# A graph network's softmax stage: ScalarE takes five of ten steps instead of four, and VectorE's product operations stand one by one between the maxima

## The reference

```python
w_m = (efeat @ W_msg + b_msg).reshape(E, 16, 16)
w_a = (efeat @ W_attn + b_attn).reshape(E, 16, 16)
h_src = feat[src][:, :, None]
e1, e2 = w_m * h_src, w_a * h_src
seg_max = segment_max(e2, dst)
ex = exp(e2 - seg_max[dst])
attn = ex / segment_sum(ex, dst)[dst]
ft = segment_sum(e1 * attn, dst).sum(axis=1)
```

## Time and profile before

| | |
|---|---|
| median of three runs | 10487.75 us |
| the profiled execution | 10485.69 us |
| its span, first to last instruction | 10482.2 us |
| busy: TensorE, VectorE, ScalarE, GpSimd | 7697.7, 7480.8, 2810.4, 8040.9 us |
| 1650 gathers `arena<-d_feat` | 3064.6 us, 1857 ns each |
| 990 products, line 1579 | 610.0 us, 678 ns each |
| 1650 forward maxima, line 1525 | 789.3 us, 478 ns each |
| 1485 sums, line 1561 | 1100.8 us, 741 ns each |
| 10560 ScalarE multiplications, line 726 | 1928.6 us, 526 ns each |

### The profile page before, as it was taken

The page is one execution under the profiler, slowest core; times in us unless marked ns, Lnnn a source line. Parts: engine busy times, 40 slices in busy tenths (PEclk is TensorE's granted clock), DMA queues, the critical chain, the costliest instruction groups (busy, mean ns, idle before and its releaser), DMA issues.

```text
span 10482.2 us, 126613 instructions
## 1 busy us (share of the span) xinstructions
PE 7697.7 (73%) x34167; PEld 3938.2 (38%) x34167; DVE 7480.8 (71%) x13704; ACT 2810.4 (27%) x12100; POOL 8040.9 (77%) x5375
## 2 busy tenths in 40 slices
PE   0899984999964666666666666617999993988884
PEld 0455542555532223322222222203555552444442
DVE  2556551444437999999999999974888872777774
ACT  0111111000005666666666666602000000000000
POOL 4788885777767888888888888753888884888887
PEclk6999996999987888887888888857999995988886
DMA  1333331222214666666666666635222221333331
GB/s 36 96 93 99 96 85 31 63 64 64 64 35 122 192 192 191 191 191 191 189 191 190 190 190 189 190 97 188 77 77 77 77 68 41 90 91 92 91 89 44
DMA packets 501017, 1210.69 MB, mean 115 GB/s; under 512 B 244715, under 2 KB 281743, under 8 KB 480135
## 3 DMA queue, kind: packets, MB, share of 16 engines
q1 hardware_dynamic: 241732, 983.55, 28.9%
q0 software_dynamic: 223712, 118.77, 9.2%
q10 hardware_dynamic: 35440, 106.85, 3.2%
HBM read 415.09 MB, written 787.23 MB: 115 GB/s over the span
## 4 chain that ended last, share of the span: by engine, by line
POOL 37%; issue 22%; PE 19%; DVE 14%; ACT 3%; DMA 2%; DVEq 1%; SPq 1%; ACTq 0%; POOLq 0%
POOL arena L513 37%; PE PS L876 11%; DVE arena L1525 4%; DVE arena L1579 4%; PE PS L1010 3%; PE PS L1011 3%; DVE arena L1529 3%; ACT arena L726 2%; DVE arena L1561 2%; PE PS L898 2%; DMA d_rel<-arena 1%; DVE arena L1539 1%; DVEq L1519 1%; DMA d_nn<-arena 0%; SPq L310 0%
## 5 line engine op out<-in xcount | busy, mean ns | idle before, releaser
L876 PE MATMUL PS<-arena,TB 125*128 125x500 bf16 (+1 forms) x17325 | 4102.2, 384 | 140.2 <-DVE arena L1275 138.3
L513 POOL DMA_INDIRECT arena<-d_feat,srci x1650 | 3064.6, 1857 | 557.8 <-issue 496.2
L513 POOL DMA_INDIRECT arena<-d_h,srci x1584 | 2026.2, 1279 | 697.6 <-issue 472.5
L876 PEld LDWEIGHTS PS<-arena,TB 125*128 125x128 bf16 (+1 forms) x17325 | 1570.0, 100 | 2363.7 <-issue 986.2
L726 ACT ACTIVATE arena<-PS,arena 125x32 f32<-125x32 f32 x10560 | 1928.6, 526 | 44.4 <-DMA arena<-d_feat,srci 44.4
L1286 DVE SCALAR_TENSOR_TENSOR arena<-arena,lane,PS 128x500 f32<-128x500 f16 x825 | 598.1, 725 | 1554.5 <-PE PS L876 1059.1
L1010 PE MATMUL PS<-arena,ident 125*125 125x512 f32 x1650 | 1087.8, 747 | 804.1 <-DVE arena L1529 802.5
L513 POOL DMA_INDIRECT arena<-d_rel,irel x858 | 1216.4, 1418 | 422.0 <-issue 261.2
L513 POOL DMA_INDIRECT arena<-d_nn,srci x858 | 1215.9, 1417 | 351.3 <-issue 261.0
L1275 DVE TENSOR_SCALAR arena<-arena,lane 125x1500 bf16<-125x1500 f16 (+1 forms) x1848 | 1188.5, 701 | 187.4 <-PE PS L876 71.8
L1561 DVE SCALAR_TENSOR_TENSOR arena<-arena 125x512 f32<-125x512 f32 x1485 | 1100.8, 741 | 0.3
(11 more groups left out here) (262 smaller groups left out, 5722.0 us busy)
## 6 DMA issues: line engine op xcount, KB each, us to landing
d_soft_den<-arena SPq DMA_DIRECT2D x330, 560.0 KB
d_soft_num<-arena SPq DMA_DIRECT2D x330, 560.0 KB
d_soft_max<-arena SPq DMA_DIRECT2D x165, 1120.0 KB
arena<-d_pick SPq DMA_DIRECT2D x99, 750.0 KB
arena<-d_lane SPq DMA_DIRECT2D x99, 750.0 KB
d_x<-arena ACTq DMA_DIRECT2D x165, 241.7 KB
arena<-d_x SPq DMA_DIRECT2D x165, 241.7 KB
d_rel<-arena SPq DMA_DIRECT2D x50, 669.4 KB
```

The costliest lines, as they stand in the source:

```text
L513: gp.indirect_dma_start(out=dst, out_offset=None, in_=table, in_offset=bass.IndirectOffsetOnAxis(ap=index, axis=0)).then_inc(S(sem), 16)
L876: ins = pe.matmul(PS[0:w, 2048 + (q % 3) * 512:2048 + (q % 3) * 512 + QW], TB[:, part, g * LANES * F:g * LANES * F + w], OH[L][i][:, g, at ...
```

## The change

ScalarE's steps are 5 to 9 instead of 6 to 9 (`GROUPS` is `(2, 2, 1)`, `AT` 5, `NA` 5). Step 4 stays with VectorE, but its results are written to `PB`, which now holds six steps per slot (`PT`, `NPB`), so that pairs of steps lie in one tile. VectorE's third group is one step: two operations of 256 elements. On VectorE, the products are issued one by one between the maxima, each group's logits with a signal of their own (`soft_at`), and `sums` begins without empty turns, after m3: the order is P, P, m0, P, m1, P, m2, P (256 wide), m3, W0, m4, carry, m5, first sum, m6, S1, m7, P (256 wide), W2, m8 and so on. On TensorE, the matmuls for ScalarE's steps stand ahead of groups 0 and 1, and those of a block's first step for ScalarE wait for all earlier steps, as five steps make two of them meet in one bank.

```diff
-GROUPS = (2, 2, 2)
+GROUPS = (2, 2, 1)
+PT = 4
+NPB = B1 - PT
...
-                    ins = act.activation(PB[:, s, n].rearrange("p a (i o) -> p i a o", i=F)[:, i], bank[:, i], ACT.Copy,
+                    ins = act.activation(PB[:, s, t - PT].rearrange("p a (i o) -> p i a o", i=F)[:, i], bank[:, i], ACT.Copy,
...
-                if not isinstance(b, int) or NA * b + n >= 2:
-                    pe.wait_ge(S("soft_ap"), NA * b + n - 1)
+                if n >= 2 or not isinstance(b, int) or b > 0:
+                    pe.wait_ge(S("soft_ap"), NA * b + max(n - 1, 0))
...
                 if left >= 1:
+                    for t in range(AT + 2, B1):
+                        scalable(b + 1, ahead, k1, t)
                     products(b + 1, ahead, k1, 0)
                     products(b + 1, ahead, k1, 1)
-                    for t in range(AT + 2, B1):
-                        scalable(b + 1, ahead, k1, t)
...
                 for n in range(MAXES):
-                    if n == 0:
-                        dve.wait_ge(S("soft_prod"), NG3 * b + NG3)
-                    else:
+                    if n:
                         dve.wait_ge(S("soft_max"), MAXES * b + n)
+                    if n < AT and n % 2 == 0:
+                        dve.wait_ge(S("soft_at"), NG3 * b + n // 2 + 1)
...
+            def product(b, s, g, a):
+                n, t, at = GROUPS[g], 2 * g, 2 * (g % 2) * 512
+                if a == 0:
+                    dve.wait_ge(S("soft_mm"), NG3 * b + g + 1)
+                to = XS[:, s, 1 + a, t:t + n, :] if t < PT else PB[:, s, t - PT:t - PT + n, a, :]
+                v.tensor_tensor(to.rearrange("p t (i o) -> p t i o", i=F),
+                                PS[0:P, at:at + n * 512].rearrange("p (t a i o) -> p t a i o", a=2, i=F, o=F)[:, :, a],
+                                GH[:, s, t:t + n, :].unsqueeze(3).broadcast_to([P, n, F, F]),
+                                ALU.mult).then_inc(S("soft_prod" if a else "soft_at"), 1)
...
-                yield
-                yield
                 weigh(0)
...
-                other = iter(()) if first and s == 0 else sums(b - 1, (s + 2) % 3)
-                for _ in maxima(b, s):
-                    next(other, None)
-                for _ in other:
+                old = iter(()) if first and s == 0 else sums(b - 1, (s + 2) % 3)
+                new = maxima(b, s)
+                product(b, s, 0, 0)
+                product(b, s, 0, 1)
+                next(new)
+                product(b, s, 1, 0)
+                next(new)
+                product(b, s, 1, 1)
+                next(new)
+                product(b, s, 2, 0)
+                for _ in range(4):
+                    next(new)
+                    next(old, None)
+                next(new)
+                product(b, s, 2, 1)
+                next(old, None)
+                for _ in new:
+                    next(old, None)
+                for _ in old:
                     pass
```

More of the change, by code:

```diff
@@ L35 @@
 ROW = 3 * CH
-AR = 35200
+AR = 36200
 KX = 6 * F + 3
@@ L206, in graph_layers @@
         SC = ar(o, 2 * CH).rearrange("p (a c) -> p a c", a=2); o += 2 * CH
-        PB_END = o + 3 * NA * 2 * CH
-        PB = ar(o, 3 * NA * 2 * CH).rearrange("p (s t a c) -> p s t a c", s=3, t=NA, a=2)
+        PB_END = o + 3 * NPB * 2 * CH
+        PB = ar(o, 3 * NPB * 2 * CH).rearrange("p (s t a c) -> p s t a c", s=3, t=NPB, a=2)
         CT = arena[:, o:o + 6 * P].rearrange("p (a c) -> p a c", a=6); o += 6 * P
@@ L217, in graph_layers @@
         W1B = arena[0:F + 1, o:o + 3 * CH].bitcast(bf16).rearrange("p (a c) -> p a c", a=3); o += 3 * CH
-        o = max(o, 32768)
-        assert PB_END <= o <= AR, o
+        o = max(o, PB_END)
+        assert o <= AR, o
         NODE = ar(0, 2 * 5 * ROW).rearrange("p (s j c) -> p s j c", s=2, j=5)
@@ L1008, in soft @@
                         t = B1 - 2 - 2 * n
-                        logits = XS[:, s, 1, t:t + 2, :] if t < AT else PB[:, s, t - AT:t - AT + 2, 0, :]
+                        logits = XS[:, s, 1, t:t + 2, :] if t < PT else PB[:, s, t - PT:t - PT + 2, 0, :]
                         pe.matmul(bank, ident[0:P, 0:P], logits, start=True, stop=False)
@@ L1522, in maxima @@
                     if n < B1:
-                        logits = XS[:, s, 1, n, :] if n < AT else PB[:, s, n - AT, 0, :]
+                        logits = XS[:, s, 1, n, :] if n < PT else PB[:, s, n - PT, 0, :]
                         prev = XS[:, s, 0, n - 1, :] if n else XS[:, (s + 2) % 3, 0, B1 - 1, :]
@@ L1537, in weigh @@
                     dve.wait_ge(S("soft_exp"), 6 * b + (B1 - t) // 2)
-                    rows = XS[:, s, 2, t:t + 2, :] if t < AT else PB[:, s, t - AT:t - AT + 2, 1, :]
+                    rows = XS[:, s, 2, t:t + 2, :] if t < PT else PB[:, s, t - PT:t - PT + 2, 1, :]
                     v.tensor_tensor(XS[:, s, 2, t:t + 2, :], rows,
                                     XS[:, s, 1, t:t + 2, :], ALU.mult).then_inc(S("soft_num"), 1)
-                yield
-                yield
                 weigh(0)
```

## The result

| kernel | runs | median, us | lowest to highest |
|---|---|---|---|
| before | 14 | 10494.67 | 10483.59 to 10501.73 |
| changed | 14 | 10523.68 | 10506.07 to 10564.55 |

The ratio is 1.0031 with an interval of 1.0022 to 1.0040: slower. The forecast was 10350, the range ended at 10455, and "slower" had a chance of 0.07. The spread has grown too: 58 us among the changed kernel's runs, 18 before.

A forecast was written before the change was run, and what follows sets the result against it. VectorE was taken to bound the softmax stage, with 21.65 of 21.96 us per block its own work. 162 x 0.87 = 141 us saved, less 2.8 at the start, net -138: 10348, median 2 above, 10350; range 10295 to 10455.

The forecast's parts named there:

- VectorE's own block: VectorE's time per softmax block without waits: 0.87 us less (0.76 to 0.95), so 20.78.
- small product: VectorE's 256-wide product for the single-step third group: 0.34 us start to start, two gaining 0.52 per block.
- maxima: On VectorE, m0 to m2 no longer follow each other directly: 0.395 us each, gain 0.25 per block.
- the extra signals: Each VectorE product has its own signal, and m2 and m4 carry a second wait: cost 0.
- The chain's middle: TensorE's moved product matmuls, before the differences, delay them but start its clock's rise sooner: 0.27 us earlier on balance.
- the mean wait at 0.31: VectorE's mean wait per block, for the exponential chain at the first weighing W0: unchanged at 0.31 us.
- ScalarE's fifth step: ScalarE's extra step, 2.80 us, before the first exponential: up to 0.4 late, covered but for about 0.1.
- the sum of 13.65: VectorE's time from maximum m10 to the next block's first weighing W0: 13.65 us, against 13.9 before.
- The start: At the stage's start ScalarE's one more step lies open: +2.8 us.
- rival A: GpSimd takes over as the bound: at 21.65 us per ten gathers the gain is 50, time 10440; chance 0.12.
- ten per 20.8: GpSimd in the new order does a block's ten gathers in 20.8 us: holds, without slack.
- a wait at a block's first product: On VectorE, a wait there for the gathers would show that GpSimd takes over.

The follow-up runs named there:

- e11: Changed kernel with all six products together at the block's start and TensorE's product matmuls in the old order: 10444.5 us, 0.9944 of the kernel before.
- e3: Changed kernel gathering only half the steps from the fourth block on (result not the reference's): 10329.2 us, 0.9839 of the kernel before.
- e4: Changed kernel plus one VectorE memset of 128 elements per block, after the third sum that follows W2: 10336.0 us, 0.9845 of the kernel before.
- e10: Changed kernel plus two memsets of 8 elements per block, among the sums: 10332.4 us, 0.9836 of the kernel before.
- e8: Changed kernel plus one memset of 8 elements per block, after the third sum that follows W2: 10336.0 us, 0.9846 of the kernel before.
- e12: Changed kernel plus one 8-element multiplication per block, both inputs in SBUF, after the third sum that follows W2: 10337.0 us, 0.9847 of the kernel before.
- e7: Changed kernel plus one 125-element multiplication per block, both inputs in SBUF, after the third sum that follows W2: 10576.7 us, 1.0074 of the kernel before.
- e9: Changed kernel plus one memset of 8 elements per block, late among the sums (behind W8): 10355.9 us, 0.9853 of the kernel before.

## Why the prediction was wrong

By its own steps:

1. VectorE's own block: forecast 20.78 (0.87 less), measured 20.75 (0.90 less). The parts: small product 0.33 start to start for 0.34, maxima 0.39 for 0.395, the extra signals nothing. Right.
2. "The chain's middle ends 0.27 earlier ... So I leave the mean wait at 0.31." TensorE's order was worth more together with the fifth step (e11: 0.46), and where no gather is held the mean wait is 0.14 to 0.16 (e3, e4, e10). Wrong by 0.15 to the pessimistic side, some 25 us.
3. ScalarE's fifth step is hidden: e3 shows it, with five steps, 20.75 in a block without waits and 0.16 of waits. It is hidden only with TensorE's new order; with the old one the waits are 0.57 a block (e11), against 0.31 before the change. (In the working, W0 to m10 has 6 maxima and not 7, which gives the 7.1 that stands there, the sum of 13.65 is 13.63, and the chances of the faster cases add to 0.89, where 0.87 stands.)
4. The start: forecast +2.8, measured +1.0.
5. The step that failed is rival A's: "ten per 20.8. It holds, without slack. If it slips to 21.65 per ten, the gain is ... 50: 10440." The mechanism had its name (GpSimd takes over) but the wrong chance, 0.12, and the wrong price. I took the longest gather of the trace, 2.81, for the longest that there can be. It was the longest of a rhythm: most gathers among the sums started at the same offset to a sum, because the one before had ended at such an offset. In the new order some start 0.13 to 0.20 into a sum, where the old trace has none, and 17 of these last until the next block's first products, 12 us. (Of the 15 held for 4.9 to 8.0 us, 8 start 0.01 into a sum, as in the old trace.) I had worked out starts of 7.6, 9.1 and 10.8 into the block; in the trace 127 gathers start at about 9.88 instead, the one of 12.09 at 9.82. "Without slack" should have been a range of its own. With 0.15 of other waits and 1.33 us of gather waits per block in place of 0 the sum becomes 20.75 + 1.48 = 22.23, slower than before.
6. I named a wait at a block's first product as the sign of A. It showed at W0, by way of ScalarE, which reads a block's rows 20.1 us, nearly one block, ahead of VectorE. The first consumer of a transfer is where its lateness shows.

That held gathers cost the time is shown (e3, e4, e8, e10, e12); why a gather is held so long is not. What stays open: which state of the two engines decides, at the same start to 0.01 us, between 1.6, 3.7 and 12.0 us. The inputs' place alone does not (e12 against e7), and no run shows a late short operation that ends a long hold (e9 has none to end). A few nanoseconds may matter: in e4 the 150 gathers that start 0.01 to 0.02 before a sum all take 1.2 us, while in the kernel before the 617 that start up to 0.02 after one take 2.2 or 2.8; but in e4 276 that start 0.01 to 0.02 after one take 1.2 too. The Trainium skill (SBUF — State Buffer, Who interferes with whom) says of VectorE's two-port modes that whoever issues first holds the shared ports for its whole instruction and blocks the other. Of an operation with two SBUF inputs it says that it contends with GpSimd's reads. Here a gather was held over 20 such operations in a row, which no single instruction's hold explains.

## What to carry to other kernels

Where two engines run at one rate, look at who is ahead: GpSimd, which waited for VectorE for about 1 us in one block of six, had little time in hand, and the longest duration in a trace in which it is locked to the other's rhythm is no bound for another order. A change that makes the one engine faster asks the same of the other. Before giving a speed-up away, relieve the coupling: here one memset of 8 elements, at 0.01 us a block, turned 1.0031 into 0.985. And when a stage's wait is found at an engine's line, follow it back through the chain until it names a transfer, and see whether the engine behind it loses its lead.

## What was unexpected in the hardware

- A gather's instruction on GpSimd lasts from 1.21 to 12.1 us with the same work, and a change of VectorE's work alone brings the longest down to 2.8 (e4); each of the 32 gathers over 4.5 us in the changed kernel ended 1.15 to 1.17 us after the start of a product, which reads PSUM: 25 after the block's first and 7 after its last, small one.
- A memset of 128 elements between dependent operations cost 0.02 us of the block, of 8 elements 0.01: less than its own 0.17 and 0.07.
- The changed kernel's time spread over 58 us in 14 runs, that of the cured one (e10) over 17 in five: that gathers are held more often in some runs than in others would fit, but only one execution of each was profiled.
